# Filler matmuls in the attention ramp, six additions and eight products moved from VectorE to GpSimd, and a shorter lead of the maxima

## What is computed

```python
def attention(x, W_q, W_k, W_v, W_o):               # 16 heads of 16 channels
    attn = softmax(0.25 * einsum('bnqd,bnkd->bnqk', q, k))
    return einsum('bnqk,bnkd->bnqd', attn, v) merged @ W_o.T
a_alpha = t @ attn_alpha_w.T
x = x + a_alpha * attention(gamma_a * rmsnorm(x) + beta_a)
f_alpha = t @ ffn_alpha_w.T
y = gamma_f * rmsnorm(x) + beta_f
return x + f_alpha * ((silu(y @ gate_w.T) * (y @ hidden_w.T)) @ out_w.T + out_b)
```

## Time and profile before

| | us |
|---|---|
| median of 3 runs | 743.63 |
| lowest, highest | 742.58, 746.47 |
| the profiled execution: its time | 742.57 |
| its span in the trace | 740.8 |
| PE busy, DVE busy, ACT busy, POOL busy | 648.9, 433.4, 392.6, 58.3 |
| mean granted clock of TensorE, share of full | 0.936 |

### The profile page before, as it was taken

How to read it: one execution, slowest core, us unless ns; L and a number is a source line. 1 busy time by engine, 2 the same in 40 slices (tenths; PEclk the granted TensorE clock), 3 DMA queues, 4 the chain that set the end, 5 groups by cost and what they waited for, 6 DMA issues and landing times.

```text
span 740.8 us, 9997 instructions
## 1 busy us (share of the span) xinstructions
PE 648.9 (88%) x3453; PEld 432.5 (58%) x3453; DVE 433.4 (59%) x862; ACT 392.6 (53%) x746; POOL 58.3 (8%) x89
## 2 busy tenths in 40 slices
PE   4766897999889988799899988899899988999896
PEld 2313676544478777444477776544588776544585
DVE  0522883877365756876364756885365647882444
ACT  1414676167774564267754573367755562468710
POOL 1004210300000003000000003000000004000000
PEclk9957899599999999799999999799999998699999
DMA  8997512420000005220000015220000023220000
GB/s 279 374 353 267 182 58 64 89 49 3 1 1 0 1 29 108 51 45 3 2 0 4 1 32 104 51 45 2 1 1 0 1 41 68 51 44 1 1 1 29
DMA packets 34483, 45.12 MB, mean 61 GB/s; under 512 B 4736, under 2 KB 27392, under 8 KB 34304
## 3 DMA queue, kind: packets, MB, share of 16 engines
q1 hardware_dynamic: 29728, 31.32, 15.1%
q0 software_dynamic: 3488, 10.49, 5.0%
q10 hardware_dynamic: 1216, 2.66, 1.3%
HBM read 28.45 MB, written 3.15 MB: 43 GB/s over the span
## 4 chain that ended last, share of the span: by engine, by line
PE 64%; DVE 11%; ACT 10%; DMA 9%; issue 3%; SPq 1%; ACTq 1%; DVEq 0%
PE psum L1234 29%; PE psum L1395 10%; PE psum L1468 8%; PE psum L1457 8%; DMA early_pieces<-in_hyp_w 3%; DVE mx L1050 3%; DMA kst<-split 2%; DMA arena<-in_hyp_w 2%; ACT arena L548 2%; PE psum L1496 1%; ACT kst L548 1%; ACT act L548 1%; PE psum L1220 1%; PE psum L1322 1%; PE psum L1480 1%
## 5 line engine op out<-in xcount | busy, mean ns | idle before, releaser
L725 ACT ACTIVATE arena<-psum 128x512 f32<-128x512 f32 x256 | 141.5, 601 | 90.0 <-PE psum L1457 88.8
L1050 DVE TENSOR_REDUCE mx<-psum 128x1 f32<-128x512 f32 x256 | 162.5, 683 | 42.4 <-PE psum L1395 42.1
L1395 PE MATMUL psum<-kst,qst 96*128 96x512 f32 x192 | 88.5, 512 | 20.9 <-DMA kst<-split 10.5
L1234 PE MATMUL psum<-act,ghw_hi 128*128 128x512 f32 (+1 forms) x288 | 89.6, 377 | 3.0 <-DVE act L851 2.5
L1457 PE MATMUL psum<-qst,kst 98*128 98x512 f32 x192 | 83.1, 453 | 1.8 <-ACT arena L725 1.8
L1395 PEld LDWEIGHTS psum<-kst,qst 96*128 96x128 f32 x192 | 43.0, 227 | 60.1 <-DVE mx L1050 35.6
L1234 PE MATMUL psum<-upw_hi,kst 128*128 128x512 f32 x256 | 72.3, 404 | 1.5 <-issue 1.5
L1468 PE MATMUL psum<-arena,vals 128*17 128x512 f32 x512 | 69.2, 613 | 1.3 <-ACT arena L725 1.0
L1234 PEld LDWEIGHTS psum<-act,ghw_hi 128*128 128x128 f32 x288 | 52.5, 190 | 15.2 <-DVE act L851 4.7
L442 POOL DMA_DIRECT2D kst<-split x36 | 17.7, 498 | 489.8 <-DMA kst<-split 407.8
L1234 PEld LDWEIGHTS psum<-upw_hi,kst 128*128 128x128 f32 x256 | 47.3, 192 | 11.3 <-issue 1.7
(11 more groups left out here) (186 smaller groups left out, 1085.7 us busy)
## 6 DMA issues: line engine op xcount, KB each, us to landing
early_pieces<-in_hyp_w SPq DMA_DIRECT2D x17, 512.0 KB, 8.2
arena<-in_hyp_w SPq DMA_DIRECT2D x15, 512.0 KB, 8.6
qst<-split SPq DMA_DIRECT2D x72, 64.0 KB, 3.4
kst<-split POOLq DMA_DIRECT2D x36, 128.0 KB, 3.5
arena<-in_x SPq DMA_DIRECT2D x4, 512.0 KB, 3.4
arena<-in_up_w POOLq DMA_DIRECT2D x8, 256.0 KB, 5.5
arena<-in_gh_w POOLq DMA_DIRECT2D x8, 256.0 KB, 3.3
out_x<-arena SPq DMA_DIRECT2D x8, 256.0 KB, 2.1
```

The lines of the kernel that those rows point to most:

```text
L725: s.activation(probs[:, kb % 2, i, :], bank[3 + n % RING], ACT.Exp).then_inc(a_p, 1)
L1050: v.reduce_max(mx[:, g % 2, col:col + 1], bank[u % RING], AX.X).then_inc(d_max, 1)
L1234: ins = pe.matmul(dst, lhs(a, c), rhs(z, c), start=start and n == 0, stop=stop and n == len(terms) - 1, skip_group_check=skip)
L1395: pe.matmul(bank[u % RING], qst[g % 3][0:KROWS, i, P * t:P * t + P], keys_of(g)[0:KROWS, i // 2, :], start=True, stop=True).then_inc(e_max, 1)
```

## The change

- Batch 0: 14 fillers ahead of the first maxima tile, one behind each of the 21 tiles of the ramp, and 4 more ahead of the first score. Batches 1 to 3: 6 fillers behind `kept_hidden(0)`, and 8 behind the tiles 14 to 20. The ones in front wait for the values to be copied out (`a_v`); the 8 wait for the third gate's silu, whose bank they write.
- `max_tiles` gives one tile less ahead of each score (31 instead of 32 by score 7 of group 0).
- The third `kept_out` moves from ahead of the first score to behind scores 2 and 3 of group 0, half at each. VectorE's `kept_output` moves from behind tile 20 to behind the tiles that stand ahead of score 3, and keeps only the two products; the two additions (`kept_x4`) go to GpSimd, ahead of `stack_k` of group 3. SP's `results` and ScalarE's first copy of heads wait for the additions; `weigh` waits for the products alone.
- `alpha_ob` and `wo_alpha` go to GpSimd (`alphas`), behind `stack_k` of group 3.
- The eight weight loads of the start share four semaphores in place of eight, so each waits for its pair.

```diff
@@ max_tiles
-            n = G * T * g + k + 1
+            n = G * T * g + k
@@ staged_in
-            return (up_in[n], 16) if n < UP else (...)
+            return (up_in[n // 2], 32) if n < UP else (...)
@@ GpSimd
+            def kept_x4(b, h):
+                pool.wait_ge(d_kept_ff, b * 2 - 1 + h)
+                pool.sem_inc(keys_free, 1)
+                pair = slice(2 * h, 2 * h + 2)
+                pool.tensor_tensor(x4_tok[:, pair, :], kept_z[:, pair, :], x4_tok[:, pair, :], ALU.add
+                                   ).then_inc(p_kept_x4, 1)
+            def alphas(b, first):
+                pool.wait_ge(d_alpha, b + 1)
+                pool.tensor_tensor(alpha_ob[:, :], alpha[:, D:2 * D], outb[:, :], ALU.mult).then_inc(p_alpha_ob, 1)
+                pool.tensor_tensor(wo_alpha[:, :, :], vow[:, :, D:2 * D],
+                                   alpha[:, 0:D].unsqueeze(1).to_broadcast([P, C, D]), ALU.mult
+                                   ).then_inc(p_wo_alpha, 1)
...
+                if not first:
+                    for h in range(2):
+                        kept_x4(b, h)
                 stack_k(b, 3)
+                alphas(b, first)
@@ VectorE
-                if not first:
-                    for h in range(2):
-                        kept_output(b, h)
...
+                        if g == 0 and k == 3 and not first:
+                            for h in range(2):
+                                kept_output(b, h)
@@ TensorE
+                pe.wait_ge(a_v, b * 2 + 2)
+                keep_clock(bank[6], 14 if first else 6)
                 for u in range(FIRST_MAX):
                     max_tile(u)
-                    if not first:
+                    if first:
+                        keep_clock(bank[6], 1)
+                    else:
...
-                    if u == FIRST_MAX - 1 and not first:
-                        kept_out(2, range(T))
+                    if u == G * T - 2 and not first:
+                        pe.wait_ge(a_kept_silu, b * KEPT)
+                    if u >= G * T - 2 and not first:
+                        keep_clock(bank[3], 2 if u == FIRST_MAX - 2 else 1)
+                if first:
+                    keep_clock(bank[6], 4)
...
                         score_tile(g, k // G, k % G)
+                        if g == 0 and not first:
+                            if k == 2:
+                                kept_out(2, (0, 1))
+                            if k == 3:
+                                kept_out(2, (2, 3))
```

More of the change, by code:

```diff
@@ L218, in build @@
             sem(n) for n in ("small_in", "params_in", "hblk_in", "vow_in", "down_in_s", "hyp_moved", "x_in")]
-        up_in = [sem(f"up_in{i}") for i in range(2 * STAGES)]
+        up_in = [sem(f"up_in{i}") for i in range(STAGES)]
         stage_in = [sem(f"stage_in{i}") for i in range(STAGES)]
@@ L243, in build @@
         d_part = sem("dve_part_out")
-        p_kept_lo = sem("pool_kept_lo")
+        p_kept_lo, p_kept_x4 = sem("pool_kept_lo"), sem("pool_kept_x4")
+        p_alpha_ob, p_wo_alpha = sem("pool_alpha_ob"), sem("pool_wo_alpha")
         e_half = sem("pe_half")
@@ L295, in staged_in @@
         def staged_in(n):
-            return (up_in[n], 16) if n < UP else (stage_in[(n - UP) % STAGES], 16 * ((n - UP) // STAGES + 1))
+            return (up_in[n // 2], 32) if n < UP else (stage_in[(n - UP) % STAGES], 16 * ((n - UP) // STAGES + 1))
         NPIECE = 2 * HP
@@ L384, in maxima_rows, with results @@
                     sp.dma_start(maxima_row(g, k), mrow[k][:, :].bitcast(F32)).then_inc(rows_in, 16)
-            def results(first_done, rows):
+            def results(added, first_done, rows):
                 for h in range(2):
-                    sp.wait_ge(d_outs, first_done + h)
+                    sp.wait_ge(added, first_done + h)
                     sp.dma_start(out[rows(h), :].rearrange("(t p) d -> p t d", p=P),
@@ L404, in batch @@
                 if not first:
-                    results(b * 2 - 1, lambda h: bass.ds(b * L - L + h * HALF, HALF))
+                    results(p_kept_x4, b * 2 - 1, lambda h: bass.ds(b * L - L + h * HALF, HALF))
                 maxima_rows(b, 1)
@@ L410, in batch @@
                 if last:
-                    results(b * 2 + 1, lambda h: bass.ds(b * L + h * HALF, HALF))
+                    results(d_outs, 1, lambda h: bass.ds(b * L + h * HALF, HALF))
             batch(0, False, first=True)
@@ L694, in heads_copy @@
                     s.wait_ge(e_pvk, b * (NG * T) + T * (g + 1))
+                    if g == 0 and not first:
+                        s.wait_ge(p_kept_x4, b * 2)
                     if g >= 2:
@@ L948, in kept_output @@
                                 ).then_inc(d_kept_ff, 1)
-                v.wait_ge(d_kept_ff, b * 2 + h - 1)
-                v.tensor_tensor(x4_tok[:, pair, :], kept_z[:, pair, :], x4_tok[:, pair, :], ALU.add
-                                ).then_inc(d_outs, 1)
             def late_weights(n):
@@ L979, in alphas @@
                     v.tensor_copy(alpha[:, :], bank[7]).then_inc(d_alpha, 1)
-                    v.wait_ge(d_alpha, b + 1)
-                    v.tensor_tensor(alpha_ob[:, :], alpha[:, D:2 * D], outb[:, :], ALU.mult)
-                    if first:
-                        v.wait_ge(vow_in, 16)
-                    v.tensor_tensor(wo_alpha[:, :, :], vow[:, :, D:2 * D],
-                                    alpha[:, 0:D].unsqueeze(1).to_broadcast([P, C, D]), ALU.mult
-                                    ).then_inc(d_woalpha, 1)
                 for t in range(T):
@@ L1130, in batch @@
                 v.wait_ge(d_x4, b * 2 + 2)
+                v.wait_ge(p_alpha_ob, b + 1)
                 v.tensor_tensor(x3_tok[:, :, :], x4_tok[:, :, :],
@@ L1465, in weigh @@
                     if kb == 0 and g == 0 and not first:
-                        pe.wait_ge(d_outs, b * 2)
+                        pe.wait_ge(d_kept_ff, b * 2)
                     for i in range(G):
@@ L1494, in attention_out @@
                         pe.wait_ge(a_onT, b * 3 + 1)
-                        pe.wait_ge(d_woalpha, b + 1)
+                        pe.wait_ge(p_wo_alpha, b + 1)
                     ins = pe.matmul(bank[1 + t // 2][:, D * (t % 2):D * (t % 2) + D], oT[:, c, P * t:P * t + P],
```

3 lines of the change are left out of this document (2 added, 1 removed).

## The result

| | before | changed |
|---|---|---|
| median, us | 745.05 | 734.52 |
| four runs of each, us | 742.58 to 747.20 | 732.64 to 737.32 |
| profiled execution, its span, us | 742.57, 740.8 | 732.64, 730.8 |
| mean granted clock of TensorE | 0.936 | 0.968 |

The ratio is 0.9879, with a 95% interval of 0.9847 to 0.9911: the changed kernel is faster by 1.2%, some 10.5 us in the medians and 9.9 in the profiled executions. The forecast was 14.8 us.

A forecast was written before the change was run, and what follows sets the result against it. TensorE was taken as the bound, slowed by half clock in the ramps, where VectorE's reduces bind nearly as much. Gains of 1.4 + 4.0 + 4.0 + 5.4 + 0 = 14.8 us from 742.57 gave 727.8 us, range 722.5 to 736.

The forecast's parts named there:

- Start: Weight loads and fillers at the kernel's start: paired loads and a possible clock change, 0.5 us either way, taken as 0.
- Batch 0: Batch 0's ramp: fillers hold the clock, turn of group 1 at 151.6 against 153.38; gain 1.8, net 1.4 us.
- Batches 1 and 2: Their ramps: additions and a wait leave VectorE, clock stays full; turn of group 1 4.4 us earlier, net 4.0 each.
- Batch 3: Batch 3's ramp: as batch 2, plus 1.4 us because fillers hold the clock at the ramp's start; net 5.4 us.
- group 1's turn is not touched: Turn of group 1: the shorter lead costs nothing there, as VectorE's row of reduces is unbroken.
- Alphas and lead: Turns of groups 2 and 3: alphas return at most 0.87 us a batch, shorter lead costs 0.58 and 0.34; put at 0.
- Rival (b): Turns of groups: the lead costs more, group 1's is not hidden, alphas bring a part; + 4, 731.8 us, chance 0.12.
- behind whose last tile no other tile stood anyway: Group 3's turn: reason given for the shorter lead costing only 0.34 us more there.
- GpSimd and SP: Additions and alphas' products on GpSimd, results and rows on SP: all finish before they are needed, cost nothing.
- Rival (e): GpSimd's operations stop VectorE for their length, 15.6 us in all: 743.4 us, no change; chance 0.03.
- Rival (d): All four ramps: clock at half with the fillers in them, batch 0 loses most; slower at 747.0 us, chance 0.04.
- a turn that comes earlier by some time brings the batch's end forward by as much: Every batch: an earlier turn of group 1 shortens the batch equally, less one tile of 0.24 us.

The follow-up runs named there:

- u_alpha: Kernel before, batches 1 and 2 written out, with only the alphas' two products on GpSimd and the paired start loads: 738.11 us, ratio 0.9941.
- u_kept: Kernel before, batches 1 and 2 written out, with only the kept work moved, additions on GpSimd and paired loads, no fillers: 731.23 us, ratio 0.9869.

## Why the forecast was 4.9 us too low

**Start (taken as 0, 0.5 either way):** the first tile came 1.50 us earlier. In the profiled executions of all kernels here it came anywhere between 128.7 and 133.5 us, with no order by kernel, so this is scatter of the start and no gain of the change; the bound of 0.5 was far too narrow. These 1.50 us of the 9.9 are luck: without them the profiled execution would have missed the forecast by 6.4.

**Batch 0 (gross 1.8):** 1.52. Fillers hidden, reduces at 0.603 us and the clock at 1.00 as laid out. The turn was named as 20.9 us behind the first tile (the times laid out there, 151.6 and a first tile at 130.9, give 20.7) and came after 21.11; with the old lead it is 20.90.

**Batches 1 and 2 (gross 4.4 each):** 4.27 and 4.06. **Batch 3 (gross 5.8):** 5.50. The turn came after 27.03, 27.03 and 27.00 us, named as 26.7. The row of VectorE that the step was built of is there: seven reduces of 0.62, two products of 0.64, then seven more. What it lacks is "group 1's turn is not touched": TensorE ends the last tile late, VectorE pauses 0.45 us, and this costs 0.35. With the old lead the number is 26.68.

The experiments also say which part each gain hangs on, which the sum did not separate: in batch 0 the fillers (20.88 with them alone), in batches 1 to 3 the moved kept work, without which the fillers leave a gap of 2.36 us and a fallen clock.

**Alphas and lead (0):** the alphas bring 0.98 us a batch where I allowed 0.87. The lead costs 0.59 at group 2 (0.58 forecast), 0.60 at group 3 (0.34 forecast) and 0.35 at group 1 (none): 1.5 instead of 0.92. Rival (b) was the right mechanism, at some 2.3 us for four batches (4 x 1.54 less 4 x 0.98) instead of its 4. At either turn the last tile needed now stands one place later, and the price is the same; for group 3 I had taken 0.34 on the ground that "behind whose last tile no other tile stood anyway".

**GpSimd and SP (0):** right. The additions take 1.25 us each, the reduces beside them 0.61, and nothing waits for them. Rival (e) falls by this row, and `u_alpha`'s and `u_kept`'s gains say the same. Rival (d) falls by the clock of 1.00 in batch 0.

**The step that failed** is the first one, "a turn that comes earlier by some time brings the batch's end forward by as much". It held across the other ends of batches, which changed by 0.3 us at most, but not across the loop's return: 5.22 us of 15.35 were lost there, to two waits for instructions of 4.13 us where there was one of 1.55, and to the half clock behind them. I had looked at what each engine does in batch 1's end and priced nothing, as nothing in it is edited. Yet the change puts 39 more matmuls into TensorE's stream ahead of the loop, and with it moves the place of every instruction behind; it also makes the loop's body 14 matmuls longer. The shifted kernels show that place alone can make or unmake the waits. That it was the 39, and not the 14, that made them here was not tried apart. The trace of before had the warning, 1.55 us of "issue" at 402.10, which the prediction doesn't name. It is no constant: written out it is 0, with four more matmuls in front of the loop 0, and in the changed kernel 4.13 with a slow clock behind.

The differences add up, from 14.7, which is the forecast's 14.8 before its terms were rounded. Ramps 1.05 less (16.4 gross against 15.35), behind the turns 0.81 less (1.77 against the 0.96 of four tiles), the loop and the other ends 5.14 less, start 1.50 more, and 0.75 that I had taken off for slips: 14.7 - 1.05 - 0.81 - 5.14 + 1.50 + 0.75 = 9.9.

## What to carry to other kernels

Where a kernel has a hardware loop, look at the jump back after every edit, also after one that only adds instructions ahead of the loop: here a wait for "issue" came and went with the loop's place, and four dummy matmuls or a written-out loop took it away. Count the packets of the instruction queues in a second pass, too. Where one engine holds another up in a critical stretch, even a short operation is worth moving to a slower idle engine: here 2 x 0.69 us a batch on VectorE became 2 x 1.25 on GpSimd, and the medians fell by some 15 us, far more than the direct 4.2. Part of that is a slow clock in some batches, whose cause stays open. And of a lead that hides a hand-over, count the places between the last piece needed and its use: one tile fewer cost 0.35 to 0.60 us at each of three turns.

## What the runs showed of the hardware

**The jump back of a loop.** TensorE stood without instructions for 1.55 us in the kernel before, 1.35 + 2.78 and 1.74 + 2.89 in two executions of the changed one, 1.41 + 2.76 in the one with the old lead, and for 0 in the two shifted ones. The shifted ones differ from the one with the old lead by matmuls of batch 0 ahead of the loop and by nothing else. The instruction queue q8 moved 9 packets from 376 to 551 us in all four executions with a wait and none in the two without.

The Trainium skill, "Runtime: NRT & Kernel Launch", Instruction fetch mechanics, says that a taken branch to a page outside the current window forces a fetch before execution can go on. The traces agree with such a stall, and that the waits and q8's packets come and go with the loop's place fits fetching by pages; which page was missing no row here shows. In these runs with the loop it was 0 to 4.6 us at the return, once as one wait, and three times as two with a single matmul between them.

**The clock behind it.** In the changed kernel the granted clock was 1.00 from 396.5 to 397.0, inside the second wait, and 0.50 from 397.5 to 403.5, and 11 matmuls took 4.87 us. Behind the single wait of 1.55 us in the kernel before the first four took 1.16 us, full speed. Behind VectorE's waits the length of the last gap does not say when the clock falls. Gaps of 2.36 us went with a fall in all three batches of the kernel with fillers alone. Of three gaps of 2.27 us in the kernel with the additions on VectorE one did (0.53 behind it), and behind the other two the clock was 1.00. A gap of 1.04 in the ramp went with a fall, gaps of 0.80 us did not, and gaps of 0.46 and 0.66 did in one kernel and not in another. What decides it stays open.
